# Output projection of a decoder layer: two sequences at once in three fp32r products, transposed and turned back, instead of fp32 one sequence at a time

## What is computed

```python
def attention(x, ctx, mask, wq, wk, wv, wo, bo):
    q = (x @ wq).reshape(b, n, H, DH).transpose(0, 2, 1, 3)
    ...
    attn = jax.nn.softmax(sim, axis=-1)
    out = jnp.einsum('bhij,bhjd->bhid', attn, v)
    out = out.transpose(0, 2, 1, 3).reshape(b, n, INNER)
    return out @ wo + bo
a = attention(x, x, tgt_mask, sa_wq, sa_wk, sa_wv, sa_wo, sa_bo)
x = layernorm(x + a, ln1_g, ln1_b)
a = attention(x, enc_output, src_mask, ca_wq, ca_wk, ca_wv, ca_wo, ca_bo)
x = layernorm(x + a, ln2_g, ln2_b)
```

## Time and profile before

| | |
|---|---|
| median of 3 runs | 501.43 us (501.26 to 502.74) |
| the profiled execution | 501.12 us, span 499.2 us |
| PE busy | 470.6 us (94%), 4644 instructions |
| DVE busy | 385.0 us (77%) |
| ACT busy | 366.8 us (73%) |
| POOL busy | 251.9 us (50%) |
| chain that ended last, output projection L582 | 10% of the span |
| mean granted TensorE clock | 0.99 |

### The profile page before, as it was taken

One profiled execution on the slowest core, in us unless ns is written; L12 is line 12 of the kernel. 1 busy time (PEld: TensorE's weight loads), 2 busy tenths in 40 slices (PEclk: granted clock), 3 DMA queues, 4 the chain that ended last, 5 costly groups with the idle time before them and its releaser, 6 DMA issues.

```text
span 499.2 us, 14097 instructions
## 1 busy us (share of the span) xinstructions
PE 470.6 (94%) x4644; PEld 431.5 (86%) x4644; DVE 385.0 (77%) x1852; ACT 366.8 (73%) x1390; POOL 251.9 (50%) x342
## 2 busy tenths in 40 slices
PE   4788999999999999999999999999999999999894
PEld 4678889999999999999999999999999997798672
DVE  4768778898888877887787777777777777538866
ACT  3547887868677788877778887777777777836763
POOL 1545357675565654555545454444554455633432
PEclk9999999999999999999999999999999999999987
DMA  8740000000000004000000000000000000400003
GB/s 242 233 195 2 1 3 1 2 2 2 1 3 1 2 2 126 1 4 1 3 1 2 2 2 1 3 1 3 3 1 3 1 2 3 169 1 0 7 13 90
DMA packets 15720, 14.18 MB, mean 28 GB/s; under 512 B 2848, under 2 KB 13344, under 8 KB 15520
## 3 DMA queue, kind: packets, MB, share of 16 engines
q1 hardware_dynamic: 14080, 12.81, 8.2%
q10 hardware_dynamic: 1568, 0.47, 0.5%
HBM read 12.10 MB, written 1.18 MB: 27 GB/s over the span
## 4 chain that ended last, share of the span: by engine, by line
PE 73%; DVE 13%; ACT 5%; issue 3%; DMA 2%; POOL 2%; SPq 1%; POOLq 0%; DVEq 0%; ACTq 0%
PE late_bank L582 10%; PE late_bank L534 10%; PE late_bank L551 10%; PE late_bank L566 10%; PE late_bank L72 8%; PE late_bank L74 8%; PE late_bank L73 8%; ACT P L817 3%; DVE P L1081 3%; DMA x<-in_xT 2%; PE late_bank L591 1%; DVE G L1198 1%; DVE ffstats L1253 1%; PE late_bank L608 1%; PE late_bank L610 1%
## 5 line engine op out<-in xcount | busy, mean ns | idle before, releaser
L817 ACT ACTIVATE P<-P,at_negmax 128x128 f32<-128x128 f32 x512 | 198.9, 396 | 79.1 <-DVE at_negmax L1081 79.1
L1530 POOL TENSOR_TENSOR P<-P,at_inv 128x512 f32<-128x512 f32 x128 | 136.6, 1078 | 123.2 <-DVE at_inv L1091 123.1
L1107 DVE COPY at_PT<-late_bank 128x512 f32<-128x512 f32 x128 | 87.7, 688 | 35.1 <-PE late_bank L534 34.9
L1081 DVE CUSTOM_DVE_ANT_0 P<-late_bank,maskb 128x128 f32<-128x128 f32 x512 | 110.5, 286 | 2.7 <-PE late_bank L551 2.7
L817 ACT ACTIVATION_READ_ACCUMULATOR P<-P,at_negmax 128x1 f32 x512 | 100.1, 195 | 0.0
L534 PE MATMUL late_bank<-ident,P 128*128 128x128 f32 x512 | 76.4, 273 | 2.0 <-DVE at_negmax L1081 1.0
L534 PEld LDWEIGHTS late_bank<-ident,P 128*128 128x128 f32 x512 | 59.8, 140 | 8.5 <-issue 4.0
L551 PE MATMUL late_bank<-at_k,at_q 64*128 64x128 f32 x1024 | 65.8, 278 | 0.9 <-DVE at_k L1099 0.9
L551 PEld LDWEIGHTS late_bank<-at_k,at_q 64*128 64x128 f32 x1024 | 59.7, 188 | 4.8 <-issue 1.2
L566 PE MATMUL late_bank<-at_PT,V 128*64 128x128 f32 x1024 | 63.0, 276 | 0.0
L566 PEld LDWEIGHTS late_bank<-at_PT,V 128*64 128x64 f32 x1024 | 55.2, 137 | 3.9
(11 more groups left out here) (195 smaller groups left out, 1055.4 us busy)
## 6 DMA issues: line engine op xcount, KB each, us to landing
ctxT_raw<-in_ctxT SPq DMA_DIRECT2D x1, 1024.0 KB, 8.8
out<-xres SPq DMA_DIRECT2D x4, 224.0 KB, 2.6
x<-in_xT SPq DMA_DIRECT2D x1, 768.0 KB, 9.5
xres<-in_x SPq DMA_DIRECT2D x1, 768.0 KB, 14.0
tap_rows<-in_short_wT SPq DMA_DIRECT2D x3, 192.0 KB, 4.9
sa_wq_raw<-in_sa_wq SPq DMA_DIRECT2D x1, 512.0 KB, 7.4
sa_wk_raw<-in_sa_wk SPq DMA_DIRECT2D x1, 512.0 KB, 8.5
sa_wv_raw<-in_sa_wv SPq DMA_DIRECT2D x1, 512.0 KB, 9.8
```

Source lines behind the costliest of these rows:

```text
L817: last = nc.scalar.activation(P[:, n % 2, h, :], P[:, n % 2, h, :], ACT.Exp, scale=-1.0, bias=negmax[:, n % 2, h:h + 1], accum_out=total[: ...
L1081: last = nc.vector.tensor_tensor_reduce(P[:, n % 2, h, :], score_bank(h), k.maskb[:, cols(n)], scale=1.0, scalar=3.0e38, op0=ALU.add, op1= ...
L1107: nc.vector.tensor_copy(PT[:, HQ * g:HQ * g + HQ, :], banks[T_BANK[g % 2]][:].rearrange("p (h l) -> p h l", h=HQ)).then_inc(pt_ok, 1)
L1530: nc.gpsimd.tensor_tensor(tile, tile, inv[:, n % 2, HQ * g:HQ * g + HQ].unsqueeze(2).to_broadcast([128, HQ, 128]), ALU.mult).then_inc(norm ...
```

## The change

The output projection now takes two sequences at once (256 columns), with the weight matrix as weights and the transposed output of P times V as the moving operand, in three fp32r products of rounded parts. The result comes out transposed (features by tokens), so ScalarE copies it to SBUF (`out_turned`), and TensorE transposes it back, one sequence at a time (`turn_back`). It is done in two halves of four chunks, 12 products each: the first at the end of odd steps, the second at the start of even steps.

For the split, ScalarE writes the high part of the first half directly and VectorE makes its low part out of PSUM (`ot_low`); the second half goes to SBUF as it is, and GpSimd makes both its parts (`split_ot`). The two weight matrices are split too: high parts by ScalarE in steps 1 and 17, low parts by GpSimd in steps 2 and 17. Residual, statistics, normalisation, gain and shift, transposes of X and its two parts now take a pair of sequences. The low parts of the second attention's weights move from steps 2, 4, 6 to 4, 6, 8. For space, the context shares memory with mixer tiles and is loaded when these are done, and ca_wo lies over self-attention weights and is loaded after their last use.

The core of the diff:

```diff
+def allocate_mixer_weights(k, mixer):
+
+    k.mixer_weights = (k.split(mixer, "w3", [128, 3, 3 * D]), k.sb(mixer, "C", [128, 2, 3, PAIR, L]),
+                       k.sb(mixer, "G", [128, PAIR, L]))
+
+
+def allocate_context(k, ctx):
+
+    k.ctxT, k.raw["ctxT"] = k.split_over_raw(ctx, "ctxT", [128, T])
...
-        OT = k.sb(ctx, "at_OT", [128, 2, H // 2, 128])
+        OT, OT_raw = k.split_over_raw(ctx, "at_OT", [128, H // 2, PCOLS])
...
+        FIRST_HALF, SECOND_HALF, NORM = -3, -4, -5
+
+        def item_pair(p, lag):
+
+            t = (p + lag) // 2
+            return t if (p + lag) % 2 == 0 and 0 <= t < PAIRS else None
...
+            sp.wait_ge(c_mm, 3 * NPAIR)
+            sp.wait_ge(y_ok, NPAIR)
             sp.dma_start(k.raw["ctxT"][:], io["ctxT"]).then_inc(ld_w["ctxT"], 16)
             sp.wait_ge(x1lo, NPAIR)
             sp.wait_ge(res1_ok, 2 * NPAIR)
-            sp.dma_start(k.wo_ca[:], io["ca_wo"].rearrange("(c p) n -> p c n", p=128)).then_inc(ld_wo, 16)
             load_feed_forward(k, sp)
+            sp.wait_ge(u_mm, 4 * NSEQ)
+            sp.dma_start(k.raw["wo_ca"][:], io["ca_wo"].rearrange("(c p) n -> p c n", p=128)).then_inc(ld_wo, 16)
...
-            def out_proj(n):
-                wait(pe, ot_ok, 2 * n + 2)
-                wait(pe, xT_lo, n - 1)
-                for c in range(H // 2):
-                    last = nc.tensor.matmul(banks[W_BANK][:, 0:128], OT[:, n % 2, c, :], out_w[att(n)][:, c, :],
-                                            start=(c == 0), stop=(c == H // 2 - 1))
+            def out_proj(t, half):
+                if t is None:
+                    return
+                pe.wait_ge((ot_lo, ot_split)[half], 2 * t + 2)
+                if half == 0:
+                    wait(pe, xT_lo, t)
+                    wait(pe, r_ok, t)
+                    wait(pe, x1lo, before(t + 4))
+                    pe.wait_ge(wo_lo, att_pair(t) + 1)
+                w = out_w[att_pair(t)]
+                for c in range(4 * half, 4 * half + 4):
+                    for wo, ot in ((w.hi, OT.hi), (w.hi, OT.lo), (w.lo, OT.hi)):
+                        last = nc.tensor.matmul(banks[W_BANK][:, 0:PCOLS], wo[:, c, :], ot[:, c, :],
+                                                start=(c == 0 and wo is w.hi and ot is OT.hi),
+                                                stop=(c == H // 2 - 1 and wo is w.lo))
                 last.then_inc(o_mm, 1)
+            def turn_back(t):
+                if t is None:
+                    return
+                pe.wait_ge(outT_ok, t + 1)
+                for b in range(PAIR):
+                    last = nc.tensor.transpose(turned_back()[:, b], outT[:, b * 128:(b + 1) * 128], k.ident[:])
+                last.then_inc(back_mm, 1)
+            def x_transpose(t):
+                if t is None:
+                    return
+                wait(pe, x_ok, t + 1)
+                wait(pe, x1lo, before(t + 5))
+                for b in range(PAIR):
+                    last = nc.tensor.transpose(banks[W_BANK][:, b * 128:(b + 1) * 128], X[:, b], k.ident[:])
+                last.then_inc(xT_mm, 1)
...
             for p in range(ITEMS):
-                x_transpose(p - 4)
                 v_half(p, 0)
+                out_proj(item_pair(p, SECOND_HALF), 1)
                 unit(p, 0)
                 transposes(p - 1, 0)
                 unit(p, 1)
+                turn_back(item_pair(p, SECOND_HALF))
                 v_half(p, 1)
                 transposes(p - 1, 1)
                 unit(p, 2)
                 x1_transposes(p, transposed_in(p))
+                x_transpose(item_pair(p, NORM))
                 if p == 0:
                     mixer_output(p, 2)
                 transposes(p - 1, 2)
                 transposes(p - 1, 3)
                 projection(p, pair_of(p, PROJECT), 1)
                 mixer_output(p, pair_of(p, OUTPUT))
-                out_proj(p - 2)
+                out_proj(item_pair(p, FIRST_HALF), 0)
                 scores(p + 1)
                 p_v(p - 1)
 
-            x_transpose(ITEMS - 4)
+            out_proj(PAIRS - 2, 1)
             transposes(ITEMS - 1, 0)
             transposes(ITEMS - 1, 1)
             pe.wait_ge(k.ff_lo, 1)
             wait_result(0)
             hidden(k, pe, 0, (0, 1))
             second_bias(0)
+            turn_back(PAIRS - 2)
             transposes(ITEMS - 1, 2)
             transposes(ITEMS - 1, 3)
-            out_proj(ITEMS - 2)
             p_v(ITEMS - 1)
-            x_transpose(ITEMS - 3)
             hidden(k, pe, 0, (2, 3))
-            out_proj(ITEMS - 1)
             wait_result(1)
             hidden(k, pe, 1, (0, 1))
-            x_transpose(ITEMS - 2)
+            x_transpose(PAIRS - 2)
+            out_proj(PAIRS - 1, 0)
+            out_proj(PAIRS - 1, 1)
             fc2_sum(k, pe, 0)
-            x_transpose(ITEMS - 1)
+            turn_back(PAIRS - 1)
             hidden(k, pe, 1, (2, 3))
             wait_result(2)
             hidden(k, pe, 2, (0, 1))
             next_fc2(1)
+            x_transpose(PAIRS - 1)
             hidden(k, pe, 2, (2, 3))
             wait_result(3)
...
+                wait(act, o_mm, 2 * (n // PAIR - 1) + o + 1)
+                tile, done = ((OT.hi, ot_hi), (OT_raw, ot_ok))[o]
+                nc.scalar.activation(tile[:, 4 * o:4 * o + 4, n % 2 * 128:(n % 2 + 1) * 128],
                                      banks[O_BANK[o]][:].rearrange("p (c l) -> p c l", c=4),
-                                     ACT.Copy).then_inc(ot_ok, 1)
...
+            def out_turned(t):
+                if t is None:
+                    return
+                act.wait_ge(o_mm, 2 * t + 2)
+                wait(act, n_ok, t)
+                nc.scalar.activation(outT, banks[W_BANK][:, 0:PCOLS], ACT.Copy).then_inc(outT_ok, 1)
...
                     exps(p, 1)
-                xT_high(p - 4)
                 v_out(p, 0)
+                ot_out(p - 2, 0)
+                out_turned(item_pair(p, SECOND_HALF))
                 q_out(p, 0)
+                ot_out(p - 2, 1)
                 mixer_normal(transposed_in(p))
-                ot_out(p - 2, 0)
-                ot_out(p - 2, 1)
                 exps(p, 2)
                 x1_high(transposed_in(p))
+                xT_high(item_pair(p, NORM))
                 q_out(p, 2)
...
+            def ot_low(n):
...
+                vec.wait_ge(ot_hi, n + 1)
+                part = np.s_[:, 0:4, n % 2 * 128:(n % 2 + 1) * 128]
+                nc.vector.tensor_tensor(OT.lo[part], banks[O_BANK[0]][:].rearrange("p (c l) -> p c l", c=4),
+                                        f32(OT.hi[part]), ALU.subtract).then_inc(ot_lo, 1)
...
                 mixer_shift(2 if p == 1 else pair_of(p - 1, OUTPUT))
-                normalise(p - 3)
+                normalise(item_pair(p, NORM))
                 reciprocals(p, 0)
                 reciprocals(p, 1)
-                xT_low(p - 4)
                 pt_out(p - 1, 0)
+                ot_low(p - 2)
                 k_out(p, 1)
+                residual(item_pair(p, SECOND_HALF))
                 pt_out(p - 1, 1)
+                statistics(item_pair(p, SECOND_HALF))
                 pt_out(p - 1, 2)
                 x1_low(transposed_in(p))
+                xT_low(item_pair(p, NORM))
                 k_out(p, 3)
                 pt_out(p - 1, 3)
                 inner_convolution(pair_of(p, CONVOLVE))
                 reciprocals(p, 2)
                 if p % 2:
                     x_low((p + PROJECT + 1) // 2)
-                if p in (2, 4, 6):
-                    weight_low(CA[p // 2 - 1])
+                if p in (4, 6, 8):
+                    weight_low(CA[p // 2 - 2])
                 elif p in (12, 13):
                     context_low(p - 12)
                 elif p == NSEQ:
                     feed_forward_low()
                 elif p == NSEQ + 2:
                     bias_low()
-                residual(p - 2)
                 reciprocals(p, 3)
                 maxima(p + 1, 0)
                 maxima(p + 1, 1)
 
-            normalise(ITEMS - 2)
-            xT_low(ITEMS - 3)
-            residual(ITEMS - 1)
-            xT_low(ITEMS - 2)
-            normalise(ITEMS - 1)
+            ot_low(ITEMS - 1)
+            normalise(PAIRS - 2)
+            xT_low(PAIRS - 2)
+            residual(PAIRS - 1)
+            statistics(PAIRS - 1)
             residual_sum(0)
+            normalise(PAIRS - 1)
             residual_moments(0)
-            xT_low(ITEMS - 1)
+            xT_low(PAIRS - 1)
             gained(0)
...
+            def split_ot(n):
...
+                pool.wait_ge(ot_ok, n + 1)
+                part = np.s_[:, 4:8, n % 2 * 128:(n % 2 + 1) * 128]
+                nc.gpsimd.tensor_copy(OT.hi[part], OT_raw[part]).then_inc(ot_part, 1)
+                pool.wait_ge(ot_part, n + 1)
+                nc.gpsimd.tensor_tensor(OT.lo[part], OT_raw[part], f32(OT.hi[part]), ALU.subtract).then_inc(ot_split, 1)
...
-                affine(p - 3)
```

(16 more changed lines are left out.)

226 lines of the change are left out of this document (127 added, 99 removed).

## The result

The changed kernel takes 518.86 us (median of 4 runs, 518.69 to 519.55), the kernel before beside it 501.35 (501.03 to 502.74): ratio 1.0345, 95% interval 1.0325 to 1.0365. It is slower by about 3.5%. The forecast was slower by 0.5%, 504.1 us, with a range to 508.5.

A forecast was written before the change was run, and what follows sets the result against it. TensorE, 94% busy, was taken to set the pace from about 85 to 413 us, VectorE after the last attention. Terms -13.6 + 8.2 - 1.0 + 9.4 = +3.0 us on 501.12 gave 504.1 us, range 498.0 to 508.5.

The forecast's parts named there:

- Term 1: TensorE's work in steps 2 to 31: projections and transposes of X fall from 61.0 to 47.4 us, -13.6 us.
- Term 2: TensorE's new waits for VectorE, in ordinary even steps and behind the maxima: 9.7 us, less 1.5 of old waits, +8.2 us.
- Term 3: Steps 30 and 31: 17.5 us together instead of 19.3, with 0.8 of the 1.8 already in Term 1, -1.0 us.
- Term 4: The tail: from the end of step 31 to the gained product 27.8 us instead of 18.4, +9.4 us.
- GpSimd at price 0: GpSimd's added copy and subtraction, 1.1 us each per sequence, cost nothing, binding only beyond about 1.7 us apiece.
- Rival 3: GpSimd's split, at 1.93 us apiece, blocks VectorE in steps 0 to 8: some 4.4 us, 508.5 us; chance 0.1.
- Rivals 1 and 2: TensorE's waits: at most 5.5 of 9.7 us, typically 498, chance 0.2; or 5.5 to 8.5 us, no change, chance 0.2.

The follow-up runs named there:

- e6: Kernel of e4 with the low part of X queued ahead of the third copy of P^T in odd steps from 11 on; 507.95 us, ratio 1.0119.
- e1: Changed kernel with the residual's statistics, from step 10 on, queued behind the last copy of P^T; 515.45 us, ratio 1.0257.
- e4: Kernel of e1 with the values product's second half moved to just ahead of the scores in even steps from 10 on; 510.58 us, ratio 1.0163.
- e12: Changed kernel, unchanged, run for one more profile; 516.17 us.
- e10: Kernel of e4 with GpSimd's rounding copy done three times in place of once; 510.57 us, ratio 1.0166.
- e2: Changed kernel with GpSimd's rounding copy of the operand's second half done three times in place of once; 522.27 us, ratio 1.0393.

## Why the prediction was wrong

- **Term 1, -13.6 us: its size was off by nearly a third.** I took the chain's 0.26 us for the lone transpose of X and 1.79 for the projection. By starts on TensorE's timeline a pair of old steps spends 2 x 1.88 on projections and 2 x 0.09 on transposes, 3.94; the new one 1.43 + 1.58 + 0.13 + 0.22 = 3.36. It saves 0.58, not 0.83: the values product starts 0.08 later where the transpose of X stands ahead of it, and then takes 0.78, for 0.80 in the new kernel without. A short instruction at a switch hides in it; its row in the chain isn't its price. e6 shows the true saving: 0.48 of 0.58 is there once both waits are gone. Over all steps that is some 3.5 us less saved than forecast.
- **Term 2, the ordinary even step, 0.25 us: the step that failed.** I wrote that "the second eight heads of the scores start at 8.66 and need the copy of T3", and never asked what the first eight need. In my own layout k was copied at 8.18 and the scores were due at 7.66: with the handing over 0.62 us of wait, not 0.25. VectorE's block began 0.24 later than laid out (3.57 after the step's start, not 3.33), which makes 0.86. I had counted 1.79 us of projection as saved and overlooked that it was also what covered the copy of k; e1 and e4 separate the two. It holds in eleven steps, not six. I missed the wait for the low part of X in ten odd steps, 0.26 us each by e6, altogether.
- **Term 2, maxima: right where the inner convolution lies ahead, wrong later.** T0 of steps 5, 7 and 9 waits 0.74, 0.74 and 1.31 us (forecast 1.2, 1.2, 2.35; in step 9 0.57 of it ahead of q); those of 13, 17 and 19 wait 0, 0.24 and 0 (forecast 0.7, 0.8, 0.7). The scores' own wait gave VectorE time there, but that this is the reason is not shown: in e4, without that wait, those of 17 and 19 are 0, and the 0.47 of step 13 comes with statistics moved ahead of the maxima. Why my layout was too dear in these steps stays open. Per ordinary pair of steps I expected -0.83 + 0.25 = -0.58 and got +0.53: 0.25 from the price, 0.61 from k, 0.26 from X low, which is the whole difference. Up to the end of step 31 the forecast is 13.1 us short: some 8 from k, 3.5 from the price, 2.6 from X low, 1.9 at the start, about 1 in steps 30 and 31, less some 4.5 that the maxima cost less than laid out. That adds up to 12.5.
- **Term 3: 1.2 us short.** Steps 30 and 31 take 18.7 us, not 17.5; that is -0.6 for a forecast of -1.8, as 0.8 of it was booked in term 1. The scores of step 30 wait 1.55 us and not 1.15.
- **Term 4, +9.4 us: the mechanism right, the size 1.6 short** (29.5 - 18.5 = 11.0 in e12), and 3.1 short in the profiled run with the lower clock. P times V came 0.2 later, the hidden products took 3.3 and not 2.85, the wait before the last projection was 1.5 and not 1.2.
- **GpSimd at price 0: right.** Copy 0.61 and subtraction 1.29 us, 1.9 in all (forecast 2.2); e10 shows that its queue has room. Rival 3 had 1.7 us apiece as its point, and two blocked VectorE operations of two SBUF inputs as its mechanism. In the changed kernel the split holds nothing up (L1216 takes 0.17 all 16 times). Other pairs of the two engines do, as before the change: the normalisation of a pair (L1224) takes 0.69 for 0.34 in three mixer steps, and a GpSimd normalisation 1.93 or more for 1.04 five times. e2 shows that the two engines do exclude each other, and where it bites first: not at the convolution but at the statistics, with a split of 3.3 us, by an operation that has a single SBUF input. The Trainium skill, page "SBUF — State Buffer", section "Who interferes with whom", names more than the two-input form that I took from it: a `tensor_scalar` on SBUF can enter a mode in which it uses both port pairs, and then contends too. By that rule, the trace agrees: in e2 and e10 the operation met the subtraction under way 17 times and was held each time (an 18th began 0.06 us before the subtraction's end and took 0.17). I had read only half of the rule.
- **Rivals and range.** Rivals 1 and 2 were both "fewer waits"; only rival 3 had more, of another cause, so the range ended at 508.5. A rival "TensorE's saved work was cover" would have stood at 504.1 + 11 x 0.6 = 511; the rest of the 518.9 is the other terms and the clock.
- **A reading.** The chain of the kernel before is not one unbroken run of matmuls from 85 to 413 us, as I wrote: at 143 to 155 and 168 to 178 it goes over VectorE and ScalarE. No term rests on it.

## What to carry to other kernels

Work that is taken off the busiest engine was also cover: for each piece removed, list what the next instruction waits for, every operand of its first part and not only of its last, and when each is ready in the new layout. An in-order queue that is 75% busy can be full just where a wait ends; the uncovered copy of k made some 7 of the 17.5 us here, and the order of the queues at the end another 7 to 8. Price a short instruction by the starts of its neighbours with and without it, never by its own row.
